# Routing a quad one step behind its transposes, and moving twelve scatters beside the experts

## What is computed

```
h = transpose(layernorm(x))
for i in range(4):
    z = layernorm_channels(h)
    y = gelu(causal_conv(z, K[i]) + z * D[i])
    out = W[i] @ y + b[i]
    h = out[:H] * sigmoid(out[H:]) + h
x1 = x + layernorm(h)
z2 = layernorm(x1)
gating = z2 @ router.T                     # 8 experts
top 2 of softmax(gating) per token
out = sum over the two: weight * (silu(z2 @ w1g) * (z2 @ w1v)) @ w2
result = x1 + layernorm(out)
```

## Time and profile before

| | |
|---|---|
| median of 3 runs | 1006.62 us |
| lowest and highest | 1004.01, 1007.06 us |
| the profiled execution | 1013.19 us |
| its span, first to last instruction | 1011.1 us |
| mean granted TensorE clock | 0.897 |
| TensorE busy (matmul) | 762.7 us, 75% |
| VectorE busy | 698.1 us, 69% |
| ScalarE busy | 487.8 us, 48% |
| GpSimd busy | 464.5 us, 46% |

### The profile page before, as it was taken

How to read it: one execution, slowest core, us unless ns; L and a number is a source line. 1 busy time by engine, 2 the same in 40 slices (tenths; PEclk the granted TensorE clock), 3 DMA queues, 4 the chain that set the end, 5 groups by cost and what they waited for, 6 DMA issues and landing times.

```text
span 1011.1 us, 23854 instructions
## 1 busy us (share of the span) xinstructions
PE 762.7 (75%) x8401; PEld 665.1 (66%) x8402; DVE 698.1 (69%) x1778; ACT 487.8 (48%) x1009; POOL 464.5 (46%) x672
## 2 busy tenths in 40 slices
PE   0029618799486994869857798676999999999991
PEld 0018518667386764857557576565899999999881
DVE  8996876759668596667966589875453335555677
ACT  7726971039610595105930169763234444563355
POOL 2102314426543365424643358665655553456560
PEclk9999859979798897979979799656999999999995
DMA  7804699992599916999089910011134444443122
GB/s 276 314 0 114 189 374 385 350 376 104 185 388 334 390 59 239 387 339 385 3 296 386 410 53 2 24 48 55 64 116 143 143 145 139 137 119 121 46 74 102
DMA packets 115519, 197.47 MB, mean 195 GB/s; under 512 B 17500, under 2 KB 38504, under 8 KB 114792
## 3 DMA queue, kind: packets, MB, share of 16 engines
q1 hardware_dynamic: 108776, 182.62, 51.1%
q0 software_dynamic: 6656, 13.64, 4.6%
HBM read 164.38 MB, written 31.85 MB: 194 GB/s over the span
## 4 chain that ended last, share of the span: by engine, by line
PE 36%; issue 25%; POOL 18%; DVE 12%; ACT 5%; DMA 2%; POOLq 1%; another core or an unknown queue 1%; SPq 0%; ACTq 0%; DVEq 0%
PE bank L1246 15%; PE bank L1263 9%; POOL zbuf L661 7%; POOL rstd_of L650 5%; PE bank L1095 3%; PE bank L1073 2%; PE bank L1218 2%; POOL sums L641 1%; DMA toep<-kernels_dram 1%; PE bank L1165 1%; POOL mean_of L646 1%; POOL m L648 1%; ACT ln_tmp L939 1%; ACT toep L950 1%; PE bank L1153 1%
## 5 line engine op out<-in xcount | busy, mean ns | idle before, releaser
L1095 PE MATMUL bank<-zbuf,toep 128*128 128x128 f16 (+3 forms) x3328 | 141.9, 204 | 94.8 <-DVE zbuf L1473 72.2
L1095 PEld LDWEIGHTS bank<-zbuf,toep 128*128 128x128 f16 x3328 | 138.7, 101 | 98.6 <-issue 48.2
L1246 PE MATMUL bank<-toep 128*128 128x256 f16 x1452 | 170.4, 274 | 7.5 <-DVE toep L1749 5.2
L1830 DVE TENSOR_TENSOR glu_work<-bank,glu_work 128x512 f32<-128x512 f32 x121 | 80.1, 688 | 136.5 <-ACT glu_work L987 94.2
L1246 PEld LDWEIGHTS bank<-toep 128*128 (+1 forms) x1452 | 141.6, 98 | 26.1 <-issue 5.2
L661 POOL TENSOR_TENSOR zbuf<-zbuf,w_cur 128x256 f32<-128x256 f32 x120 | 90.1, 752 | 141.5 <-DVE zbuf L1537 141.4
L987 ACT ACTIVATE glu_work<-bank 128x512 f32<-128x512 f32 x121 | 68.5, 596 | 162.3 <-PE bank L1246 142.0
L1130 PE MATMUL bank<-wo_cur,glu_work 128*128 128x256 f32 x512 | 134.8, 408 | 2.5 <-ACT glu_work L884 2.2
L1537 DVE TENSOR_REDUCE zbuf<-bank 128x256 f32<-128x512 f32 x128 | 87.0, 687 | 69.9 <-PE bank L1095 69.9
L721 POOL DMA_INDIRECT z_sorted<-toep x104 | 102.1, 982 | 65.6 <-PE bank L1246 32.1
L1130 PEld LDWEIGHTS bank<-wo_cur,glu_work 128*128 128x128 f32 x512 | 96.3, 198 | 44.3 <-issue 17.3
(11 more groups left out here) (266 smaller groups left out, 1369.8 us busy)
## 6 DMA issues: line engine op xcount, KB each, us to landing
toep<-kernels_dram SPq DMA_DIRECT2D x104, 1024.0 KB, 14.0
glu_work<-kernels_dram SPq DMA_DIRECT2D x16, 1024.0 KB, 14.1
toep<-z_sorted SPq DMA_DIRECT2D x73, 128.0 KB
y_sorted<-toep SPq DMA_DIRECT2D x73, 128.0 KB
toep_last<-kernels_dram SPq DMA_DIRECT2D x8, 1024.0 KB, 14.1
z_sorted<-ln_tmp SPq DMA_DIRECT2D x2, 3584.0 KB, 26.8
hres<-in_x SPq DMA_DIRECT2D x1, 4096.0 KB, 12.8
toep<-in_x SPq DMA_DIRECT2D x1, 4096.0 KB, 22.2
```

Of the source, the lines that this page charges most:

```text
L1095: last = MM(dst[:, d * (B // 4):, :], toep_slot(g)[:, c, d * P:(d + 1) * P, k], z_conv[:, 0:QUADS - d * (B // 4), g * GROUP + c].rearrange ...
L1246: last = MM(out[:, piece % 2 * XP:(piece % 2 + 1) * XP], w1_row[:, pw, weights_at(s, piece * P, P)], xT_s[:, px * XP:(px + 1) * XP], start ...
L1830: TT(inner[:, s.at % 4, :], bank[3 + s.at % 2 * 2][:, :], gate_act[:, s.at % 2, :], ALU.mult).then_inc(s_inner, 1)
```

## The change

The router's matmuls of a quad are put one step of TensorE's list later, so that the next quad's transposes stand ahead of them; the choices and with them the places and counts follow by one step (`CHOOSE_AT` becomes 13, 19, 24, 26 and `PLACE_AT` 15, 21, 26, 28; `dense_low` stays where it was). The number of scatters that wait for transposes falls from 36 to 24, which is the whole of segment 0, the first three waiting for the ninth quad's transposes and the last three for the sixteenth's; the other 80 are woven into the expert stage. On GpSimd all scatters stand behind `h_moments(7)`.

```diff
-    CHOOSE_AT.append(max([_q + 10] + PLACE_AT[-1:]))
+    CHOOSE_AT.append(max([_q + 11] + PLACE_AT[-1:]))
...
+IN_QUADS = 24
...
-                    if transfers[0] >= 36:
+                    if transfers[0] >= IN_QUADS:
                         in_burst((BEFORE + FIRSTS[g] - 6) // 2 * 2 + 2)
                     elif transfers[0] % 3 == 0:
-                        pool.wait_ge(s_z2T, min(6 + transfers[0] // 3, QUADS))
+                        pool.wait_ge(s_z2T, min(QUADS - IN_QUADS // 3 + 1 + transfers[0] // 3, QUADS))
...
             h_moments(6)
-            scatter(0, 0, 4)
             h_moments(7)
-            scatter(0, 4)
+            scatter(0)
...
-            for q in range(QUADS + 10):
+            for q in range(QUADS + 11):
                 if q + 1 < QUADS:
                     forward(q + 1)
-                if q >= 10:
+                if 10 <= q < QUADS + 10:
                     z2_transpose(q - 10)
                 if q < QUADS:
                     weights(q)
-                if 10 <= q:
-                    route(q - 10)
+                if 11 <= q:
+                    route(q - 11)
```

## The result

The changed kernel takes 1009.02 us, the median of 20 runs (1004.47 to 1013.62), against 1005.62 us for the kernel before in 20 runs taken beside it (1000.64 to 1007.06). The ratio is 1.0041 [1.0027, 1.0055]: slower by some 4 us (3.4 by the two medians), a little more than the 0.3% that I called measurable. The forecast was 1010.0.

The account below looks back on a forecast made before the run. Latency between engines was taken to bound the routing stage, TensorE the experts. Router +3.3 us, with -0.8 for quads 12 to 15 inside it, and experts +0.1 make +3.4 on 1006.62: median 1010.0 us, range 1003.5 to 1013.5.

Parts of the forecast that it names:

- part 1: Routing matmuls' 8.7 us wait for ScalarE's copy: removing it gains 0 for quads 6 to 9, 0.8 us on three later quads.
- the ring: Cycle of transposes, ScalarE's copy and normalizations pacing the quads; from quad 11, 3.33 us a quad without the wait, not 3.61.
- Part 2: First choice and its places one VectorE step later: quad 5's copy starts 2.2 us earlier, lost again at quad 8's normalization; sum 0.
- Part 3: Second choice one step later: starts 4.05 us later, the last moments end 2.5 later, quad 14's transposes start 1.2 later.
- Part 4: Third choice one step later: starts 3.9 us later, 0.6 saved on a low part; first expert product +3.3 us.
- Part 5: Moved scatters, and loads and gathers in the experts: nearly free, experts +0.1 us (0 to 1.5).
- B: Experts also wait, tile 19 and the sums of quads 0 and 2 stalling TensorE: +6 to +8 us, 1014; chance 0.15.
- C: Near nothing: TensorE's issue gaps in the counts not met, clock rises one product earlier; about +1 us, 1007.6; chance 0.2.
- D: Faster: TensorE's clock holds at 2.4 GHz through routing as an idle gap is partly filled; -4.3 us, 1002.3; chance 0.15.

Follow-up runs that it names:

- e0: The kernel before, unchanged, timed and profiled a second time; ratio 1.0003 to the kernel before.
- e5: The changed kernel with VectorE's low halves of the expert weights put behind the moments of the later quads; ratio 1.0050 to the kernel before.
- e7: The changed kernel with quads 0 to 8 routed in their own step and the first two choices where they were; ratio 1.0021 to the kernel before.
- e3: The changed kernel with only the last quad of each choice routed in its own step, choices, counts and places as before; ratio 1.0040 to the kernel before.
- e2: The kernel before with only the scatters moved as in the change, routing and choices as before; ratio 0.9991 to the kernel before.
- e8: The kernel before, unchanged, profiled a third time on a third chip, where its median is 1016.19 us.
- e11: The kernel before with scatters moved, low weight halves behind the moments, and a dense quad's low part ahead of places and choose; ratio 1.0007 to the kernel before.

## Why the prediction was right

**The reading of the waits (part 1)** held. TensorE's 8.7 us of waits for ScalarE's copy gave nothing up to quad 9, where the ring goes through z(q+1). Where they were on the path, from quad 12 on, the ring came down to 3.33 us, as worked out (679.43 - 676.10 and 682.77 - 679.43), from 3.5 in e0 (T(14) - T(13) = 69.63 - 66.12): 0.2 us a quad where I had 0.28.

**Part 2, sum 0,** held in its steps. glu(12) waited 0.81 us for tanh (forecast 0.85), the copy of quad 5 waited 2.21 instead of 4.37 us, and T(6) came 2.1 us earlier (31.25 against 33.39). All of it was lost at m(2), for which z(8) waited 2.48 us: T(8) is at 43.12 and was at 43.13.

**Part 3** held with sizes a little too large. choose(1) came 3.81 us later than in e0 (forecast 4.05), m(3) 2.25 (2.5), and T(12) 2.26 later. I had forecast instants from the first profile, in which T(12) was late by 0.6 us of a gap in count(1). e5 is the direct proof of the link: 2.28 us taken from in front of m(3) came out as 2.18 at T(12) and 2.19 at choose(2).

**Part 4, the mis-sized term.** The forecast put choose(2) 3.9 us later; against e0 it is 4.37, since R(13) behind T(14) (its cost as forecast) adds to a full delay of 2.26 at T(12). And it took 12.34 us from choose(2) to choose(3). That figure was of a disturbed profile: places(2) there had waited 3.96 us where 2.25 is the clean number. Clean, it is 10.93 in e0 and 10.41 in the changed kernel, where R(15) no longer stands ahead of choose(3). So choose(3) came 3.85 us later, minus 0.6 for the low part, and the sum is 3.24 where I had 3.3. The error in the first term and that in the second nearly cancel; that the total agrees to 0.1 us is partly luck, that its sign is right, and that the delay at choose(2) is half from choose(1) and half from R(13) (2.26 and 2.11 us by e7), is not.

**Part 5** held on the chip of e0 to e3. e2 measures the scatters at -0.02 us in F, 0.3 us behind it and 0.9991 in time. No transpose of a sorted tile (L1218) waited in the changed kernel. VectorE waited once for a gather, 2.2 us where I had 2.0:

```profile
DVE zbuf L1874 <- DMA zbuf<-y_sorted,toep: 2.2, 1, 2.2
```

and TensorE didn't feel it (20.00 of 20 us busy from 862 to 882). The load of tile 19, where the Trainium skill's figure for a DMA ("DMA: Bandwidth & Descriptors", section "Anatomy of one DMA — SWDGE (gpsimd) path") and the 3.7 us of the earlier trace rows would have differed by 0.8 us, didn't stop TensorE. That section is on DMAs that GpSimd issues, and this load is issued by SP. The two can't be told apart by this, as the cover may have been larger than I reckoned; the first four loads of sorted tiles in e0, also of 128 KB, landed in 2.7 us (median), between the two. On the other two chips part 5 failed: I had put the last gathers at nothing because their sum comes later, and the kernels with moved scatters lost 2.3 to 3.7 us behind F.

**The rivals.** B, a wait of the experts for a load or a gather, wasn't seen in the measured pair. On the third chip the total, 5.7 us, is nearly B's size, by another wait than B names. C supposed that the gaps in the counts would not be met. The profiled execution of the changed kernel indeed has none, and by the profiles alone (89.11 against 88.17) the change costs 0.9 us, just as C says; but neither does the clean kernel before have any, and the medians differ by 3.4. The 0.9 us is thus an artefact of one profile. D came nearest to deciding: T(6) was free of the fall, 0.66 us long after 3.03 us of idle time, but T(7) ran 1.11 us after 2.93 us more of it, and the granted clock stayed near 0.5 up to the experts. The first 48 products took 8.04 us, and 7.15 before. The idle time that the change took from one quad came back ahead of the next.

## What to carry to other kernels

A wait on the busiest-looking pair of engines is worth only what the ring through it is worth: ask what the waiting engine would do next, and who releases that. When work is put a step later to hide a wait, look for the decision that hangs on the last piece of it; here four choices hang on one quad each, and the delays of the second (3.81 us) and the third (4.37) came to 3.24 at the first product. A time ratio that is larger than the stretch under study explains points at another stretch: count that one too, on every chip. Take a second profile of the old kernel before sizing anything by a stretch of one, and count from a common instant.

## What the runs showed of the hardware

**A stall of 2 to 4 us that no semaphore explains.** Between count(2) and places(2), 2.15 us by work, the runs had 2.15 (e0 to e3 and the changed kernel), 3.85 (first profile of before) and 4.3 to 6.4 us (all eight runs on the two other chips). On these the kernel before took 1016 to 1018 us instead of 1006; most of that lies behind the first product (316.6 us in e8 against 307.2 in e0). TensorE shows it as "issue" between matmuls of a count, VectorE as a wait for a remote engine. What it is stays open: instructions fetched from memory late and transfers that get in the way are candidates, and none was tried.

**A wait at the end that comes with the chip and the order of the gathers.** 1.85 to 2.44 us of VectorE in all six profiles with moved scatters on two chips, none in three such profiles on the first (the changed kernel, e2, e3) and none in the five with the scatters as before; told behind e11.

**The same kernel isn't one number.** The runs of before lie around 1001.5 and around 1006 us, on one chip, and the profiled T(0) between 605.4 and 611.4. A difference of 3 us can be seen in medians of 10 to 20 runs (the intervals here reach 0.14 to 0.32% to either side) and not in one.

**A DMA held back by a VectorE instruction.** A scatter takes 0.96 us on GpSimd, but one that starts while L1700 runs on VectorE can take as long as that has still to run and more. On GpSimd of the changed kernel, the one beside L1700 (667.08, 2.28 us) and an ordinary one:

```profile
667.25 2.94 POOL L722 DMA_INDIRECT z_sorted<-toep  x1 [0.31 <-issue]
...
691.81 0.96 POOL L722 DMA_INDIRECT z_sorted<-toep  x1 [0.30 <-issue]
```

It ended 0.83 us after L1700 did. In the first profile of before, a scatter that started at 674.63, within the second L1700 (673.84, 2.28 us), took 2.32 us and also ended 0.83 us after it. Not every one is held: the scatter at 674.29 of the changed kernel started 0.01 us after the second L1700 and took 0.96. It didn't cost any time in the measured pair: kernels of both orders have it, and e2's F is that of e0.

**The clock rises at another product from profile to profile.** The first 48 products at the start of the experts took 7.15, 7.75 and 8.04 us (before, e0, after), though the products are the same: the granted clock was 0.50 for the first 3 us in before and for the first 4 in e0 and after, in whose fifth it was 0.87 and 0.57, and full or nearly so from there. Why it differs isn't shown; e0 and before run the same kernel.
